# Where the three parts of dt are summed in the recurrence: on VectorE in SBUF, or in TensorE's accumulator

## What is computed

```python
u = jax.nn.silu((xc + conv_b[:, None]).transpose(0, 2, 1))
x_dbl = u @ W_x.T
dt = jax.nn.softplus(x_dbl[..., :dt_rank] @ W_dt.T + b_dt)
Bs = x_dbl[..., dt_rank:dt_rank + D_STATE]
Cs = x_dbl[..., dt_rank + D_STATE:]
A = -jnp.exp(A_log)
...
    dA = jnp.exp(dt_t[..., None] * A)
    h = dA * h + (dt_t * u_t)[..., None] * B_t[:, None, :]
    return (h, jnp.einsum('bdn,bn->bd', h, C_t))
```

## Time and profile before

| | us |
|---|---|
| median of 3 runs | 780.83 (779.65 to 781.97) |
| the profiled execution | 788.52 |
| its span, first to last instruction | 786.7 |
| PE busy | 670.7 |
| DVE busy | 572.5 |
| ACT busy | 439.7 |
| POOL busy | 459.0 |

### The profile page before, as it was taken

One profiled execution on the slowest core, in us unless ns is written; L12 is line 12 of the kernel. 1 busy time (PEld: TensorE's weight loads), 2 busy tenths in 40 slices (PEclk: granted clock), 3 DMA queues, 4 the chain that ended last, 5 costly groups with the idle time before them and its releaser, 6 DMA issues. The chain is left out here.

```text
span 786.7 us, 9488 instructions
## 1 busy us (share of the span) xinstructions
PE 670.7 (85%) x2977; PEld 327.4 (42%) x2977; DVE 572.5 (73%) x590; ACT 439.7 (56%) x659; POOL 459.0 (58%) x239
## 2 busy tenths in 40 slices
PE   3878798898998998998989999988883689999981
PEld 1323333333433333433333343457650146777720
DVE  3488998999899999899999995544741436666542
ACT  1887667568568576675784651634551125555420
POOL 6359999999999999899999995500000000000000
PEclk9999999999999999999999999989996989999996
DMA  3389566666666765665675750000000000000002
GB/s 94 80 258 306 198 256 231 222 230 222 213 237 202 247 235 195 234 229 201 250 238 196 260 191 26 1 1 2 2 1 14 8 12 2 1 2 2 2 1 60
DMA packets 32739, 105.45 MB, mean 134 GB/s; under 512 B 6677, under 2 KB 7326, under 8 KB 32670
## 3 DMA queue, kind: packets, MB, share of 16 engines
q1 hardware_dynamic: 31702, 103.94, 38.8%
q10 hardware_dynamic: 648, 0.55, 0.4%
q0 software_dynamic: 320, 0.13, 0.1%
HBM read 98.84 MB, written 2.10 MB: 128 GB/s over the span
## 5 line engine op out<-in xcount | busy, mean ns | idle before, releaser
L1472 POOL TENSOR_TENSOR hc<-hh_all,cc 128x1024 f32<-128x1024 f32 x128 | 299.0, 2361 | 8.4 <-PE py L638 3.7
L638 PE MATMUL py<-hc,w_cst 128*128 128x512 f32 x512 | 243.2, 603 | 2.3 <-DVE yg L1276 1.4
L1268 DVE TENSOR_TENSOR_SCAN hh_all<-da,pb 128x1024 f32<-128x1024 f32 x72 | 164.6, 2287 | 2.5
L638 PEld LDWEIGHTS py<-hc,w_cst 128*128 128x128 f32 x512 | 97.7, 193 | 104.8 <-issue 77.5
L1268 DVE TENSOR_TENSOR_SCAN hh_all<-pb,dbu 128x1024 f32<-128x1024 f32 x56 | 127.7, 2281 | 15.1 <-POOL dbu L1483 9.9
L1483 POOL TENSOR_TENSOR dbu<-bb,dtu_all 128x1024 f32<-128x1024 f32 x56 | 132.3, 2362 | 0.0
L1015 ACT ACTIVATE pb<-dt_all,w_aneg 128x1024 f32<-128x1024 f32 x56 | 62.5, 1116 | 54.1 <-DVE hh_all L1268 52.5
L1263 DVE TENSOR_TENSOR pb<-pb,dtu_all 128x1024 f32<-128x1024 f32 x72 | 87.5, 1215 | 5.1 <-PE pb L627 4.0
L1015 ACT ACTIVATE da<-dt_all,w_aneg 128x1024 f32<-128x1024 f32 x72 | 80.5, 1137 | 0.5
L627 PE MATMUL pb<-bc,w_sel 128*128 128x512 bf16 x144 | 44.2, 389 | 31.2 <-DVE hh_all L1268 28.8
L1762 POOL MEMSET wa<- 128x128 f32 x4 | 0.6, 212 | 90.0 <-POOLq L370 90.0
(11 more groups left out here) (288 smaller groups left out, 980.3 us busy)
## 6 DMA issues: line engine op xcount, KB each, us to landing
cc<-scr SPq DMA_DIRECT2D x128, 512.0 KB, 4.2
bb<-scr SPq DMA_DIRECT2D x56, 512.0 KB, 4.7
w_xs<-hc SPq DMA_DIRECT2D x6, 256.0 KB, 4.6
w_xst<-in_x SPq DMA_DIRECT2D x2, 512.0 KB, 6.3
scr<-bcf SPq DMA_DIRECT2D x8, 128.0 KB, 4.1
w_xs<-dt_all SPq DMA_DIRECT2D x4, 256.0 KB, 6.3
w_xs<-dtu_all SPq DMA_DIRECT2D x4, 256.0 KB, 6.6
out<-yy SPq DMA_DIRECT2D x4, 256.0 KB, 4.0
```

What stands on the lines that cost most here:

```text
L638: nc.tensor.matmul(py[:, half(h)], ident, hc[u % NHC][:, half(h)], start=(n == 0), stop=(n == NS - 1)).then_inc(hc_used, 1)
L1268: nc.vector.tensor_tensor_scan(hh[u % NHH][:, :], decay[:, :], drive[:, :], 0.0, ALU.mult, ALU.add).then_inc(scan_done, 1)
L1472: nc.gpsimd.tensor_tensor(hc[u % NHC][:, :], hh[u % NHH][:, :], cc[u % NCC][:, :], ALU.mult).then_inc(hc_done, 1)
```

## The change

VectorE adds `rl` to the gap in `ex` after it has made the gap. It waits on a new semaphore for its own previous result. TensorE adds only `ex` to the logarithm. The computed value is the same sum in another order.

```diff
-        scr_in = sem("scr_in")
+        scr_in, gap_done = sem("scr_in"), sem("gap_done")
...
         def pe_dt_add(pe, s, h):
             pe.wait_ge(ln_done, 2 * s + h + 1)
-            nc.tensor.matmul(px[h][:, :], ident, ex[:, half(h)], start=False, stop=False, skip_group_check=True)
-            nc.tensor.matmul(px[h][:, :], ident, rl[:, half(h)], start=False, stop=True,
+            nc.tensor.matmul(px[h][:, :], ident, ex[:, half(h)], start=False, stop=True,
                              skip_group_check=True).then_inc(px_full[h], 1)
...
         def dve_lost(dve, s, h):
             dve.wait_ge(one_done, 2 * s + h + 1)
             nc.vector.scalar_tensor_tensor(ex[:, half(h)], px[h][:, :], 1.0, ex[:, half(h)],
-                                           ALU.add, ALU.add).then_inc(lost_done, 1)
+                                           ALU.add, ALU.add).then_inc(gap_done, 1)
+            dve.wait_ge(gap_done, 2 * s + h + 1)
+            nc.vector.tensor_tensor(ex[:, half(h)], ex[:, half(h)], rl[:, half(h)], ALU.add).then_inc(lost_done, 1)
```

## The result

The changed kernel takes **795.7 us** (median of 4 runs, 794.9 to 796.7), the kernel before 781.4 in the same job (4 runs, 779.7 to 785.0). The ratio is 1.0177, with an interval from 1.0138 to 1.0216: slower by 14.3 us.

What follows compares the result with a forecast made beforehand. GpSimd was taken to pace the loop, 425 of 434 us. One boundary at 2.1 us and six at 3.1 gave 20.7 us, added to 780.8 for 801.5 us; range 783 to 830.

Steps and rivals of the forecast that it cites:

- the ring: At sequence boundaries: GpSimd's drive of unit 10, scans 10 to 13, TensorE's backlog, sums, scan of unit 3, GpSimd.
- TensorE's relief costed at nothing: 16 matmuls removed, 1.7 us per sequence: TensorE would only wait that much longer for the scan of unit 13.
- faster* rival: At the boundaries TensorE's saved 1.7 us per sequence reaches GpSimd, at most 5.6 us won: 775 us, chance 0.04.
- The prologue at nothing: Two of the 16 additions, 1.4 us together, cost nothing, since VectorE waits 2.58 us for ScalarE afterwards.
- Each waits for the other's running operation: Loop additions and GpSimd operations exclude each other in turns; 20.7 us in all, 801.5 us, chance 0.60.
- no collision* rival: Only the additions' own time counts in the loop: 0.77 us per boundary, 4.6 us at six, 785 us, chance 0.15.
- the step: Sequence 3's two additions: first delays scan 10 by 0.6 us, second waits too; product of unit 11 comes 3.1 us later.
- the three half-clock stretches: TensorE at 1.2 GHz behind its wait at every second boundary, 1.7 us each; losing all three gives 16.5 us.
- 1.0 of room: At the first boundary GpSimd takes the scan of unit 3 late anyway, so 3.1 - 1.0 = 2.1 us there.
- GpSimd's wait at unit 3 grows to 2.1: Expected sign at the boundary: GpSimd's wait for the scan of unit 3 grows from 0.43 to about 2.1 us.
- My sign of being wrong: Wrong if TensorE's wait for the scan of unit 13 does not grow, or the boundaries do not move with it.
- Starving: VectorE's loop addition is let in only when GpSimd runs dry: up to 10 us per boundary, 815 to 850 us, chance 0.15.

Runs made afterwards that it cites:

- dve_only: The changed kernel with both TensorE matmuls kept, so the relu part counts twice; 803.0 us, ratio 1.0295 to the kernel before.
- product_first: The changed kernel with the second half's addition moved behind VectorE's product of unit 11; 803.7 us, ratio 1.0272 to the kernel before.

## Why the prediction was right or wrong

- **GpSimd paces the loop, and the ring decides at the boundaries: right.** Each boundary moved with the scan of unit 13, at 2 to 3 and 4 to 5 with the distance kept at 22.85 us, and what the intervals grew by adds up to 14.8 us of the loop's 15.1.
- **TensorE's relief costed at nothing: right**, 428.8 us of loop without the matmul and 429.5 with it. The *faster* rival falls with it. I had TensorE wait 1.7 us longer for the scan of unit 13 without the matmul; it waits 0.6 to 0.7 longer (0.88 us for 0.21 at 4 to 5), and the rest goes into other waits. With both matmuls kept beside the additions the kernel is 6 to 7 us slower, and the rows put that down to where the half-clock stretches fell; four boundaries are the same to 0.03 us.
- **The prologue at nothing: right.** Its two additions take 0.69 us each, and the wait for ScalarE that I named shrank from 2.58 us to 1.14.
- **Each waits for the other's running operation: right as a mechanism.** The PSUM operand takes it away (no wait in 16 records). That version costs 5.3 us over before, about the 4.6 that the *no collision* rival had computed. The rule of the Trainium skill that I had weighed (page "SBUF — State Buffer", section "Who interferes with whom") agrees in its direction. Its "whole instruction" doesn't in size, if the record is taken for the instruction: an addition of 0.69 us delays GpSimd by 0.43 us.
- **Where the step failed: the sizes of the two waits.** I let the first addition start at the drive's end and take its 0.69 us from there, and delay GpSimd by 0.69. Measured, it ends 0.54 us after the drive, some 0.15 us sooner, and GpSimd loses 0.43. So scan 10 starts 0.47 us behind the drive's end (248.56 - 248.09), not 0.64 (243.84 - 243.20), and the second addition's wait is 1.55 us, not 1.8. Together **2.70 us per boundary, not 3.1**: 7 x 0.4 = 2.8 us of the 5.6 by which the loop's 15.1 fell short of 20.7.
- **The other half is the clock.** I left the three half-clock stretches behind the scan of unit 13 where they were, and gave 16.5 us as the end if they go. They went, which I hadn't forecast as the likely case. One on the ring cost 1.59 us at 3 to 4 (21.11 - 19.52), where I had 1.7. By my own figure of 1.4 for each, these boundaries should grow by 2.7 - 1.4 = 1.3 us, and grew by 1.1 to 1.2. The first boundary got one: 2.7 - 1.0 of room + 1.7 = 3.4, measured 3.5. With both corrections, made after the result, the sum is 3.4 + 3 x 2.7 + 3 x 1.3 = 15.4, where the loop shows 15.1 and the medians 14.3.
- **GpSimd's wait at unit 3 grows to 2.1: wrong in the place.** It stayed 0.43. The loss shows one step ahead, before `py`.
- **My sign of being wrong, that TensorE's wait for the scan of unit 13 doesn't grow: it came true at five of the seven boundaries**, where it grew by 0.15 us at most. It is 2.15 us for 2.14 at 3 to 4 and 0.32 for 0.21 at 4 to 5; the boundaries moved all the same, so the sign was badly chosen. These are the five with a half-clock stretch some 8 us ahead, which makes TensorE's work before the wait longer. In `dve_only`, which has no stretch ahead of these two scans, the same waits are 3.60 and 1.56 us. The change at 4 to 5, then `dve_only` at both:

```profile
319.63 0.61 PE L626 MATMUL pb<-bc,w_sel 128*128 128x512 bf16 x2 [0.32 <-DVE hh_all L1269]
```

```profile
269.11 0.60 PE L627 MATMUL pb<-bc,w_sel 128*128 128x512 bf16 x2 [3.60 <-DVE hh_all L1270]
...
323.89 0.60 PE L627 MATMUL pb<-bc,w_sel 128*128 128x512 bf16 x2 [1.56 <-DVE hh_all L1270]
```

- **Starving: not here.** It is no fancy, since a copy met it, but 0 of the 14 additions did.

What I can't tell is why a copy collides and a reduction doesn't, what let one copy miss its turn, and what makes a stretch at half clock come at one boundary and not at the next; no run held the clock fixed.

## What to carry to other kernels

Beside a GpSimd that is almost never idle, the price of a VectorE addition with both inputs in SBUF isn't its own duration but the phase of its wait. With one operand in PSUM it took 0.69 us each time; with both in SBUF it took up to a GpSimd operation more, depending on when it was issued. The profile books the wait as busy time, so compare the least and the most of one form. Work taken off an engine just ahead of a wait was worth nothing here, even on the busiest one. And if shifts of a few us matter, look at where the half-clock stretches of TensorE fell in both traces before you explain the remainder.

## What the runs showed of the hardware

- Two SBUF inputs aren't the only condition: a 128x512 fp32 copy within SBUF waits for GpSimd too (0.84 and 1.98 us for 0.43), a reduction of the same tile doesn't (0.686 us, 16 of 16).
- Turns alternate: of two additions in a row each waited for one GpSimd operation (5.34 us for both). The exception is one copy of 14, which waited for three more (7.75 us); for 56 additions there was none.
- The records aren't wholly exclusive: GpSimd lost 0.43 us to an addition of 0.69, and 0.17 to a copy of 0.43, and an addition ends 0.54 us after the GpSimd record ahead of it, less than its own 0.69. Whether the work itself overlaps or only the beginnings and ends of records, the traces don't tell.
- Stretches with the clock granted at 0.50 (1.2 GHz, some 3.3 us, twice that at a few places) changed their boundary in nearly every version. One directly behind TensorE's wait for the scan of unit 13 cost 1.59 us at 3 to 4; ahead of the wait it cost nothing that the intervals show (22.85 us behind the scan in all, 58.1 us in the change and in `dve_only`). `product_first` has the change's 17.9 us from scan 9 to scan 13, and takes 7 to 8 us more with the stretches behind it.
